# Score matmuls of the second layer written as two 64-column halves per bank

## The reference, cut to what matters

```python
h = lorentz_linear(x, W, b, scale)          # 4096 x 64
q = lorentz_linear(h, Wq, bq, scale_q)
k = lorentz_linear(h, Wk, bk, scale_k)
qm = jnp.concatenate([-q[:, :1], q[:, 1:]], axis=-1)
att = 2.0 + 2.0 * (qm @ k.T)
att = jax.nn.sigmoid(att / att_scale + att_bias)
att = adj * att
support = att @ h
```

## Time and profile before

| | us |
|---|---|
| median of 3 runs | 1082.35 |
| the three runs | 1079.66, 1082.35, 1089.49 |
| span of the profiled execution, first to last instruction | 1078.1 |
| median of the runs less that span | 4.25 |
| second layer's loop, first score matmul to last | 295.9 to 541.1 |

### The profile page before, as it was taken

The page is one execution under the profiler, slowest core; times in us unless marked ns, Lnnn a source line. Parts: engine busy times, 40 slices in busy tenths (PEclk is TensorE's granted clock), DMA queues, the critical chain, the costliest instruction groups (busy, mean ns, idle before and its releaser), DMA issues.

```text
span 1078.1 us, 14786 instructions
## 1 busy us (share of the span) xinstructions
PE 1028.7 (95%) x5391; PEld 445.2 (41%) x5410; DVE 865.4 (80%) x1012; ACT 768.9 (71%) x808; POOL 254.3 (24%) x140
## 2 busy tenths in 40 slices
PE   6999999999799999999989998999999998989998
PEld 2333333337633333334334443444544554436544
DVE  7999989997777666797669987887789887898781
ACT  4555555554666566686698999888888888997682
POOL 1089000000001000003025464443433433440010
PEclk9999999999899999999989999999999999999999
DMA  9989999991067888787754445555555545446451
GB/s 350 401 329 422 379 333 306 366 384 57 2 232 262 279 282 281 240 284 260 250 168 156 130 127 185 183 173 178 168 170 171 174 140 175 136 138 219 141 169 40
DMA packets 96342, 238.33 MB, mean 221 GB/s; under 512 B 16400, under 2 KB 45072, under 8 KB 79888
## 3 DMA queue, kind: packets, MB, share of 16 engines
q1 hardware_dynamic: 87056, 220.62, 60.1%
q10 hardware_dynamic: 9216, 16.78, 4.1%
HBM read 219.55 MB, written 17.83 MB: 220 GB/s over the span
## 4 chain that ended last, share of the span: by engine, by line
PE 76%; DVE 10%; ACT 9%; issue 4%; DMA 1%; SPq 0%; DVEq 0%; ACTq 0%
PE PS L568 52%; PE PS L744 5%; PE PS L745 5%; PE PS L880 4%; PE PS L849 4%; ACT work L1250 2%; ACT work L1258 2%; DVE work L2057 2%; DVE work L2045 1%; DVE ring L2063 1%; ACT work L1261 1%; ACT work L1175 1%; DVE work L2051 1%; PE PS L580 1%; ACT work L1244 1%
## 5 line engine op out<-in xcount | busy, mean ns | idle before, releaser
L1717 DVE TENSOR_TENSOR work<-work,ring 128x1024 f32<-128x1024 f32 x128 | 152.4, 1231 | 71.5 <-ACT work L1175 71.5
L1175 ACT ACTIVATE work<-PS,att_sc 128x1024 f32<-128x1024 f32 x128 | 147.8, 1202 | 80.8 <-PE PS L745 71.9
L1100 ACT ACTIVATE work<-PS 128x1024 uint8<-128x1024 f32 x128 | 124.0, 1021 | 107.1 <-PE PS L568 105.3
L568 PE MATMUL PS<-ring,work 128*65 128x256 f32 (+1 forms) x600 | 190.7, 465 | 3.9 <-DVE work L2084 3.8
L546 POOL TENSOR_TENSOR ring<-work,ring 128x1024 f32<-128x1024 f32 x57 | 135.9, 2384 | 236.4 <-DVE work L2057 236.3
L568 PE MATMUL PS<-work 128*64 128x512 f32 (+2 forms) x800 | 153.5, 525 | 1.1 <-ACT work L1244 1.0
L2051 DVE SCALAR_TENSOR_TENSOR work<-PS,work 128x1024 f32<-128x1024 f32 x72 | 88.0, 1223 | 54.3 <-PE PS L568 45.9
L568 PEld LDWEIGHTS PS<-ring,work 128*65 128x65 f32 x600 | 80.6, 138 | 90.9 <-issue 65.4
L744 PE MATMUL PS<-work 128*128 128x512 f16 x256 | 98.6, 385 | 2.3 <-DVE work L1470 1.3
L1250 ACT ACTIVATE work<-work 128x1024 f32<-128x1024 f32 x72 | 76.0, 1055 | 34.4 <-DVE work L2045 34.3
L745 PE MATMUL PS<-work 128*128 128x512 f16 x256 | 97.8, 382 | 0.0
(11 more groups left out here) (271 smaller groups left out, 1457.0 us busy)
## 6 DMA issues: line engine op xcount, KB each, us to landing
ring<-in_adj_t SPq DMA_DIRECT2D x96, 1024.0 KB, 5.4
ring<-in_adj_t SPq DMA_DIRECT2D x104, 512.0 KB, 4.1
work<-in_adj_t SPq DMA_DIRECT2D x32, 1024.0 KB, 8.5
codes<-work ACTq DMA_DIRECT2D x64, 256.0 KB, 7.4
ring<-codes SPq DMA_DIRECT2D x64, 256.0 KB, 3.9
H<-in_adj_t SPq DMA_DIRECT2D x24, 512.0 KB, 4.1
X<-in_x SPq DMA_DIRECT2D x2, 256.0 KB, 4.6
X<-in_x SPq DMA_DIRECT2D x1, 512.0 KB, 10.0
```

What stands on the lines that cost most here:

```text
L568: return mm(out_ap, lhsT, rhs, start=starts, stop=True, skip_group_check=True)
L1100: nc.scalar.activation(made[:, k, u * UNIT:(u + 1) * UNIT], PS[:, (4 + 2 * u) * BANK:(6 + 2 * u) * BANK], ACT.Relu).then_inc(sem("codes_ma ...
L1175: nc.scalar.activation(att[:, u, :], PS[:, (4 + 2 * u) * BANK:(6 + 2 * u) * BANK], ACT.Sigmoid, bias=att_sc[:, 2:3], scale=att_sc[:, 1:2]) ...
L1717: V.tensor_tensor(prob[:, m % 4, :], att[:, u, :], ring[:, s % RING, u * UNIT:(u + 1) * UNIT], ALU.mult)\
```

## The change

It replaces the two matmuls of a bank by four. The 128 key columns of the stationary tile are cut in two halves e = 0 and 1 of 64 columns; the first half goes to partitions 0 to 63 of the bank, the second to partitions 64 to 127 (`half_rows(e)` is `slice(e * 64, (e + 1) * 64)`). Both halves stream the same 512 columns of `q_hh`, then both those of `q_ll`. The numbers computed are the same.

```diff
@@ -741,8 +741,10 @@
                 for c in range(2):
                     i0 = h * HALF + u * UNIT + c * BANK
                     o = PS[:, (4 + 2 * u + c) * BANK:(5 + 2 * u + c) * BANK]
-                    mm(o, k_hl[:, jt * P:(jt + 1) * P], q_hh[:, i0:i0 + BANK], start=True, stop=False)
-                    ins = mm(o, k_hl[:, jt * P:(jt + 1) * P], q_ll[:, i0:i0 + BANK], start=False, stop=True)
+                    for qs, first in ((q_hh, True), (q_ll, False)):
+                        for e in range(2):
+                            ins = mm(o[half_rows(e), :], k_hl[:, jt * P + e * D:jt * P + (e + 1) * D], qs[:, i0:i0 + BANK],
+                                     start=first, stop=not first)
                 ins.then_inc(sem("scores_ready"), 1)
```

## The result

| | us |
|---|---|
| changed kernel, median of 4 runs | 1071.57 (1070.45 to 1072.81) |
| before, the runs of the same set | 1084.86 (1079.66 to 1089.49) |
| ratio, with its 95% interval | 0.9894 (0.9859 to 0.9928) |
| predicted | 1069.85 (1065 to 1077) |
| span of the profiled execution | 1071.1, in a run of 1072.81 |

The account below looks back on a forecast made before the run. PE was taken to bound the second layer's loop. Removing 58 border pairs of 0.25 us gives 14.5, less 1.0 at ACT's stretches and 1.0 at DVE's: 12.5 under 1082.35, so 1069.85 us, range 1065 to 1077.

Parts of the forecast that it names:

- two surcharges of 0.15 and 0.10: Second layer's plain step: PE pays 0.15 us going from 128 to 64 columns and 0.10 going back, together 0.25.
- rival 1: Score matmul behind a gather: the 0.10 belongs to new f16 weights, only 0.15 goes; 7.5 us gained, time 1074.85; chance 0.13.
- Pairs cost what one matmul costs: Second layer's scores: two 64-column matmuls with their weight loads take 0.216 us, as one 128-column matmul; nothing added.
- Rival 2: Pairs of halves in the 64 steps: weight loads no longer hide, costing 56 us against 12.5 gained; time about 1126; chance 0.03.
- 58 of 62 pairs of borders: Loop steps 1 to 62: four with 128-column visitors (5, 35, 56, 59) save nothing; 58 x 0.25 = 14.5 us.
- 1.0 for ACT's stretches and 1.0 for DVE's: Gain lost in the loop: 1.0 us where ACT is twice the chain, 1.0 behind both, where DVE is nearly full.
- DVE is nearly full: Behind ACT's two stretches: DVE busy 18.53 of 18.74 and 14.73 of 15.04 us; loss between nothing and 1.7, taken as 1.0.
- Rival 3: Steps 37 to 50 all DVE's: 14 steps lose 0.25 us each, 11.0 gained, time 1071.4; chance included in the forecast's 0.80.
- 12.5 us: Second layer's loop: net gain, 14.5 - 1.0 - 1.0; first to last score matmul shrinks from 245.2 to about 232.7 us.
- 1069.85 us: Whole kernel: forecast time, span 1065.6 plus 4.25 us around it, 12.5 under the median before of 1082.35.
- Everything behind 541 us keeps its length: Layers behind the second layer's loop: they start earlier by the gain and keep their own length.

Follow-up runs that it names:

- half_first: Changed kernel with only unit 0's score matmuls in 64-column halves, unit 1 full width as before the change: 1082.40 us, ratio 1.0009.
- the two interleaved kernels: Kernel before and changed kernel, each with PE order scores 0, gather 0, scores 1, gather 1: 1103.22 us (ratio 1.0195) and 1076.92 us (0.9958).
- visitors: Changed kernel with the four 128-column visitors in the loop (lines 722, 580, 768, 773) also written as 64-column halves: 1070.88 us, ratio 0.9892.
- The runs without roots: Kernel before and changed kernel, ACT's two square roots and table loads in the loop replaced by writing zeros: fourteen steps took 51.79 and 48.23 us.

## Why the prediction was right

- *PE sets the step, and two surcharges of 0.15 and 0.10 stand in it.* Right, to 0.01: the step fell by 0.26 and not 0.25. half_first and the two interleaved kernels show that they go with the column shape and not with the type or the wait; rival 1 is out.
- *Pairs cost what one matmul costs.* Right: 1.73 us for sixteen. Rival 2, and the rule behind it, is out for f16 as well: the loads take 110 ns each and hide beside pairs of 0.216 that use all 128 rows.
- *58 of 62 pairs of borders.* Right: from before to the changed kernel steps 5, 35, 56 and 59 get shorter by no more than 0.07 us, and visitors gets back 0.23 to 0.36 at each of them.
- *1.0 for ACT's stretches and 1.0 for DVE's.* Right in kind, too small in sum: 2.6 us of the gain are lost in the fourteen steps. The loss under ACT's stretches grew from 1.1 to 2.05, so by 0.9, where the prediction had 1.0. Behind them, on DVE's chain, it grew from nothing to 1.7, where the prediction took 1.0 between bounds of 0 and 1.7: the upper one was the measured one. What it had wrong is the reason: "DVE is nearly full" reads the stretch as full of DVE's own work. The runs without roots show that this work has room in a step of 3.44 us; DVE was full from catching up, so both terms hang on ACT's stall. Rival 3, with all 3.5 lost, isn't what happened, although the median of 1071.57 lies next to its 1071.4.
- *12.5 us.* The loop is 12.1 us shorter in both profiles of the changed kernel; 58 x 0.26 - 2.6 = 12.5 by its terms. Most of the 0.4 is the start of the loop, at the 1.2 GHz level: steps 0 and 1 together take 7.49 us before and 7.53 after, so that the 0.26 of step 1 doesn't show.
- *1069.85 us.* That the time came out so near is in part luck. The medians differ by 13.3 in the first set, 9.0 in the second, and by 9.4 to 10.8 between runs of the same group, less than the loop's 12.1. That spread isn't the loop's: a spell at 1.2 GHz ahead of it, worth 6 us, comes in some executions, and the one profile of before, which has none over the degree sums, gave no warning of it. "Everything behind 541 us keeps its length" held but for 0.5 us in the third layer and a second, shorter spell at about 970. Why the changed kernel keeps 1 to 2 us less than its loop gains, group by group, stays open.

## What to carry to other kernels

Count the borders between column shapes in PE's stream, not only the matmuls: each change of shape costs 0.10 to 0.15 us here, so work that alternates between 128 and 64 columns gains from being written in one shape, while halving only a part moves the borders and gains nothing. Before such a change pays elsewhere, see how far the next engine is behind PE: in the first layer DVE's own step was 0.36 us under PE's, and 0.10 after the change, too little to make up for its other work, and POOL's cast waited until DVE stopped. When another engine looks full, ask whether it is full of work or of catching up; leaving out the stall in front of it tells.

## What the hardware showed that I had not expected

- Halves need not be neighbours with a shared operand: lower, lower, upper, upper ran at the same 1.73 us. Thirty-two quarters run in 1.73 us too, beside their surcharge.
- A GpSimd cast of 128 x 384 took 35, 51 and 87 us in three kernels beside a busy DVE, ending each time 0.36 us after DVE's first gap, and a like one 0.5 us beside an idle one. POOL, which made PE wait with the 87 us, is busy for 24% of the span in the kernel before.
- The same program ran the degree sums at 2.4 GHz in one execution and the greater part of them at 1.2 GHz in another, 6 us apart. What sets it off stays open.
